# Routing work of a mixture-of-experts block at other places: ranks made at the output projection, logits and picks earlier, the late list in two pieces

## The reference

```python
sa, ca, ga, sb, cb, gb = (mod[:, 0], mod[:, 1], mod[:, 2], mod[:, 3], mod[:, 4], mod[:, 5])
ga = (2 * (ga >= 0) - 1) * jnp.maximum(jnp.abs(ga), 0.25)
gb = (2 * (gb >= 0) - 1) * jnp.maximum(jnp.abs(gb), 0.25)
h = _layernorm(x, axis=-1) * (1 + ca) + sa
x = x + ga * _L0_attn_ref(h, L0_attn_wq, L0_attn_bq, L0_attn_wk, L0_attn_bk, L0_attn_wv, L0_attn_bv, L0_attn_wo, L0_attn_bo)
h = _layernorm(x, axis=-1) * (1 + cb) + sb
x = x + gb * _L0_ffn_ref(h, L0_ffn_gate, L0_ffn_experts_w1, L0_ffn_experts_w2, L0_ffn_experts_w3)

def _L0_ffn_ref(x, gate, experts_w1, experts_w2, experts_w3):
    router_logits = jnp.einsum('bsh,he->bse', x, gate)
    routing_weights, selected = jax.lax.top_k(router_logits, TOP_K)
    routing_weights = jax.nn.softmax(routing_weights, axis=-1)
    onehot = jax.nn.one_hot(selected, E, dtype=x.dtype)
    tok_w = jnp.einsum('bsk,bske->bse', routing_weights, onehot)
    g = jnp.einsum('bsh,ehi->ebsi', x, experts_w1)
    u = jnp.einsum('bsh,ehi->ebsi', x, experts_w3)
    hid = jax.nn.silu(g) * u
    eo = jnp.einsum('ebsi,eih->ebsh', hid, experts_w2)
    return jnp.einsum('ebsh,bse->bsh', eo, tok_w)
```

## Time and profile before

| | us |
|---|---|
| median of 3 runs | 359.72 |
| lowest and highest | 357.95, 360.33 |
| profiled execution | 359.48 |
| its span, first to last instruction | 357.7 |
| mean granted clock of TensorE | 0.906 |
| TensorE, VectorE, ACT, GpSimd busy | 287.2, 217.1, 183.1, 164.9 |

### The profile page before, as it was taken

The page is one execution under the profiler, slowest core; times in us unless marked ns, Lnnn a source line. Parts: engine busy times, 40 slices in busy tenths (PEclk is TensorE's granted clock), DMA queues, the critical chain, the costliest instruction groups (busy, mean ns, idle before and its releaser), DMA issues.

```text
span 357.7 us, 7283 instructions
## 1 busy us (share of the span) xinstructions
PE 287.2 (80%) x2264; PEld 209.4 (59%) x2264; DVE 217.1 (61%) x554; ACT 183.1 (51%) x393; POOL 164.9 (46%) x262
## 2 busy tenths in 40 slices
PE   3478899999998978979785359959789999999800
PEld 2134455555554544545432149959789999999800
DVE  5668778788889796888761515882313334433227
ACT  7422476757675763656461235524526666666400
POOL 4140235455655594858649513765613333333310
PEclk9999699999999998999787659987969999999965
DMA  3932282524335342220103121543243545445355
GB/s 91 174 66 65 66 193 57 161 82 147 106 104 158 104 164 67 60 69 16 32 15 90 54 59 38 158 126 107 87 125 97 153 125 165 138 136 158 94 187 180
DMA packets 57255, 38.23 MB, mean 107 GB/s; under 512 B 5240, under 2 KB 52104, under 8 KB 57216
## 3 DMA queue, kind: packets, MB, share of 16 engines
q1 hardware_dynamic: 52880, 31.16, 32.3%
q0 software_dynamic: 2272, 4.69, 3.9%
q10 hardware_dynamic: 2064, 1.91, 2.1%
HBM read 23.58 MB, written 6.75 MB: 85 GB/s over the span
## 4 chain that ended last, share of the span: by engine, by line
PE 45%; DVE 18%; issue 12%; POOL 10%; DMA 8%; ACT 4%; ACTq 1%; SPq 1%; POOLq 0%; DVEq 0%
PE psA L1469 15%; PE psB L1479 8%; DVE negm L916 5%; PE psA L1296 4%; PE psO L1341 4%; PE psB L1321 4%; POOL xs_d L702 3%; PE psM L1276 2%; DMA y_d<-ys,qs 2%; PE psA L1299 2%; DMA xs_d<-pay,dest 2%; POOL probs L642 2%; DMA qs<-xs_d 2%; DVE xn L837 1%; PE psM L1365 1%
## 5 line engine op out<-in xcount | busy, mean ns | idle before, releaser
L480 ACT ACTIVATE probs<-psB 128x512 f32<-128x512 f32 x128 | 71.2, 594 | 35.0 <-PE psB L1321 34.7
L916 DVE TENSOR_REDUCE negm<-psA 128x4 f32<-128x1024 f32 x64 | 78.0, 1222 | 18.2 <-PE psA L1299 17.4
L1469 PE MATMUL psA<-qs,kd 128*128 128x128 f32 x624 | 81.4, 288 | 0.0
L1469 PEld LDWEIGHTS psA<-qs,kd 128*128 128x128 f32 x624 | 78.3, 204 | 0.0
L768 POOL DMA_INDIRECT y_d<-ys,qs x39 | 37.5, 962 | 77.7 <-ACT ys L552 73.2
L1169 DVE TENSOR_TENSOR qs<-psA,kd 128x512 f32<-128x512 f32 x39 | 26.9, 690 | 67.8 <-PE psA L1469 63.1
L642 POOL TENSOR_SCALAR_AFFINE_SELECT probs<-probs 128x512 f32<-128x512 f32 x64 | 39.1, 636 | 37.2 <-ACT probs L480 37.1
L1296 PE MATMUL psA<-kd,qs 96*128 96x512 bf16 x128 | 50.0, 412 | 1.7 <-DVE negm L916 1.5
L1321 PE MATMUL psB<-qs,kd 98*128 98x256 bf16 x256 | 47.3, 285 | 0.7 <-ACT probs L480 0.6
L1479 PE MATMUL psB<-kd,qs 128*128 128x128 f32 x312 | 43.7, 285 | 4.5 <-DVE qs L1169 4.0
L1479 PEld LDWEIGHTS psB<-kd,qs 128*128 128x128 f32 x312 | 40.0, 201 | 5.0 <-DVE qs L1169 5.0
(11 more groups left out here) (187 smaller groups left out, 344.8 us busy)
## 6 DMA issues: line engine op xcount, KB each, us to landing
kd<-in_L_ffn_experts_w_dram SPq DMA_DIRECT2D x39, 256.0 KB, 2.9
w_sb<-in_L_ffn_experts_w_dram SPq DMA_DIRECT2D x8, 512.0 KB, 4.5
kd<-parts SPq DMA_DIRECT2D x96, 32.0 KB
qs<-parts SPq DMA_DIRECT2D x42, 64.0 KB
mod_sb<-mod_d SPq DMA_DIRECT2D x8, 320.0 KB, 4.7
qs<-xs_d SPq DMA_DIRECT2D x39, 65.0 KB, 1.9
pay<-pay SPq DMA_DIRECT2D x8, 128.0 KB
probs<-y_d SPq DMA_DIRECT2D x3, 256.0 KB, 4.5
```

The costliest lines, as they stand in the source:

```text
L480: nc.scalar.activation(probs[:, kt, n % PRING], psB[:, kt, :].rearrange("p (h q) -> p h q", h=H2), ACT.Exp).then_inc(s["exped"], 1)
L916: nc.vector.tensor_reduce(negm[:, b % 2, :, :, j], psA[:, n % 2].rearrange("p q (h k) -> p q h k", h=H2), AX.X, ALU.max, negate=True).then ...
L1469: last = nc.tensor.matmul(ps[:, k * P:(k + 1) * P], w[:, r, k * P:(k + 1) * P], xsT[:, r], start=True, stop=True)
```

## The change

- rank_rows of sequences 0 to 3 is called inside project_out at pair 1 of steps 5 to 8, ahead of the projection's own matmuls, with other columns of the same bank (480 on; the count 496 on). Its reader is waited for together with the projection's. VectorE runs gate_attn first, then place_rows.
- In steps 6 and 7 logits are issued at pair 3 instead of 6; VectorE copies them and makes the two maxima at pair 4 and the rest (now picks) at pair 6, instead of all at pair 7. In step 8 the logits of sequence 4, its top2 and picks come at pair 2.
- The two pick instructions become one.
- GpSimd in step 8 issues put_rows of sequence 3 at pairs 2 to 5 and two of sequence 4 at pairs 6 and 7; two are left behind the loop, where five were. Between the tiles the puts come in another order around each scatter, the last of them behind scatter(8) instead of before scatter(9).
- late_list is cut in two: late_tiles at tile 6, the rest at tile 7, instead of all at tile 5.
- fill_blanks goes from step 1 to step 6 on SP.

```diff
-            return late(b)[:, 2 * E:4 * E]
+            return late(b)[:, 480:480 + 2 * E]
...
-                if step == 1:
+                if step == 6:
                     fill_blanks()
...
-                    if step == B and j in (2, 4, 6):
-                        put_rows(3, (j - 2) // 4, j // 2 % 2 ^ 1)
+                    if step == B and 2 <= j <= 5:
+                        put_rows(3, (j - 2) // 2, j % 2)
+                    if step == B and j >= 6:
+                        put_rows(4, 0, j % 2)
...
-            put_rows(3, 1, 1)
-            put_rows(4, 0, 0)
+            put_rows(4, 1, 0)
             pad_term(B - 1)
-            put_rows(4, 0, 1)
+            put_rows(4, 1, 1)
             x1_sum(B - 2)
-            put_rows(4, 1, 0)
             ln2_rstd(B - 2)
-            put_rows(4, 1, 1)
             h2_scale(B - 2)
...
+                if n == 4:
+                    weights_pow(B - 2)
+                if n == 5:
+                    weights_pow(B - 1)
                 if n == 3:
                     put_rows(B - 3, 0, 0)
...
-                if n == 8:
-                    put_rows(B - 1, 0, 1)
-                if n == 9:
-                    put_rows(B - 1, 1, 1)
-                scatter(n)
...
                 if n == 8:
                     put_rows(B - 1, 1, 0)
+                scatter(n)
...
+                if n == 7:
+                    put_rows(B - 1, 0, 1)
+                if n == 8:
+                    put_rows(B - 1, 1, 1)
...
+
+            def picks(b):
                 tt = slice(2 * b, 2 * b + 2)
...
-                for k in range(TOPK):
-                    nc.vector.tensor_tensor(pick[:, k, tt], iota_e[:].rearrange("p (o e) -> p o e", o=1).broadcast_to([P, 2, E]),
-                                            topf[:, tt, k:k + 1].broadcast_to([P, 2, E]), ALU.is_equal).then_inc(s["picks_ready"], 1)
+                nc.vector.tensor_tensor(pick[:, :, tt], iota_e[:].rearrange("p (o q e) -> p o q e", o=1, q=1).broadcast_to([P, TOPK, 2, E]),
+                                        topf[:, tt].rearrange("p t (k o) -> p k t o", o=1).broadcast_to([P, TOPK, 2, E]),
+                                        ALU.is_equal).then_inc(s["picks_ready"], 2)
...
-                    if j == 1 and 5 <= step < B:
-                        place_rows(step - 5)
                     if j == 1 and has(step - 3):
                         gate_attn(step - 3)
+                    if j == 1 and step >= 5:
+                        place_rows(step - 5)
...
-                    if j == 7 and step < B and has(step - 4):
+                    if j == (7 if step <= 5 else 4) and step < B and has(step - 4):
                         logits_copy(step - 4)
                         top2(step - 4)
+                    if j == (7 if step <= 5 else 6) and step < B and has(step - 4):
+                        picks(step - 4)
...
-                    if j == 0 and step == B:
-                        place_rows(3)
+                    if j == 2 and step == B:
                         logits_copy(4)
-                    if j == 2 and step == B:
                         top2(4)
+                        picks(4)
...
                 if n == 5:
                     place_rows(B - 1)
+                if n == 6:
+                    late_tiles()
+                if n == 7:
                     late_list()
...
-            def project_out(b):
+            def project_out(b, ranked=None):
+
                 if b == 0:
                     pe.wait_ge(s["wo_in"], 32)
-                take_late(b, ("t1_ready", 2 * b + 2))
+                if ranked is None:
+                    take_late(b, ("t1_ready", 2 * b + 2))
+                else:
+                    take_late(b, ("t1_ready", 2 * b + 2), ("rank_read", ranked + 1))
+                    rank_rows(ranked)
...
-                    if j == 1 and 5 <= step < B:
-                        rank_alone(step - 5)
                     if j == 1 and has(step - 3):
-                        project_out(step - 3)
+                        project_out(step - 3, step - 5 if step >= 5 else None)
...
-                    if j == 6 and step < B and has(step - 4):
+                    if j == (6 if step <= 5 else 3) and step < B and has(step - 4):
                         logits(step - 4)
-                    if j == 0 and step == B:
-                        logits(4, 3)
+                    if j == 2 and step == B:
+                        logits(4)
```

More of the change, by code:

```diff
@@ L227, in rank_at @@
         def rank_at(b):
-            return late(b)[:, 2 * E:4 * E]
+            return late(b)[:, 480:480 + 2 * E]
         def count_at(b):
-            return late(b)[0:1, 4 * E:5 * E]
+            return late(b)[0:1, 496:496 + E]
         xs_in = [sem(f"xs_in{r}") for r in range(XRING)]
@@ L812, in _ @@
                     put_rows(B - 1, 1, 0)
+                scatter(n)
+                if n == 3:
+                    put_rows(B - 3, 0, 1)
+                if n == 4:
+                    put_rows(B - 3, 1, 1)
+                if n == 5:
+                    put_rows(B - 2, 0, 1)
+                if n == 6:
+                    put_rows(B - 2, 1, 1)
+                if n == 7:
+                    put_rows(B - 1, 0, 1)
+                if n == 8:
+                    put_rows(B - 1, 1, 1)
         @block.vector
@@ L1095, in early_list, with late_tiles @@
                 list_done(nc.vector.tensor_tensor(taken[:, 1, 0:E], taken[:, 0, E:], taken[:, 0, E - 1:2 * E - 1], ALU.subtract))
-            def late_list():
+            def late_tiles():
                 up_to(1, count_at(B - 1))
@@ L1103, in late_list @@
                 list_done(nc.vector.tensor_tensor(tile_jump[:], tile_base[:, 1:], tile_base[:, 0:E], ALU.subtract))
+            def late_list():
                 tile_list(NEARLY, NLATE, tile_jump[:])
@@ L1191, in _ @@
             top2(B - 3)
+            picks(B - 3)
             for n in range(NTILE):
@@ L1208, in _ @@
                     top2(B - 2)
+                    picks(B - 2)
                 if n == 4:
@@ L1211, in _ @@
                     top2(B - 1)
+                    picks(B - 1)
                     place_rows(B - 2)
@@ L1378, in rank_rows @@
                 if count:
-                    nc.tensor.matmul(late(b)[:, 4 * E:5 * E], ones_b[:], before[:, 2 * b + 2], start=True, stop=True).then_inc(s["count_ps"], 1)
+                    nc.tensor.matmul(late(b)[:, 496:496 + E], ones_b[:], before[:, 2 * b + 2], start=True, stop=True).then_inc(s["count_ps"], 1)
                 nc.tensor.matmul(rank_at(b), tri[:], used[:, 2 * b:2 * b + 2].rearrange("p t e -> p (t e)"), start=True, stop=False)
@@ L1382, in rank_rows, with logits @@
                                  start=False, stop=True).then_inc(s["rank_ps"], 1)
-            def logits(b, ranked=None):
+            def logits(b):
                 pe.wait_ge(s["h2T_ready"], b + 1)
-                if ranked is None:
-                    take_late(b, ("lg_ready", b + 1))
-                else:
-                    take_late(b, ("lg_ready", b + 1), ("rank_read", ranked + 1))
+                take_late(b, ("lg_ready", b + 1))
                 for t in range(2):
@@ L1393, in logits @@
                 last.then_inc(s["lg_ps"], 1)
-                if ranked is not None:
-                    rank_rows(ranked)
             def rank_alone(b, count=False):
```

10 lines of the change are left out of this document (removed).

## The result

| | before | after |
|---|---|---|
| median of 4 runs, us | 359.51 (357.95 to 360.33) | 343.29 (342.39 to 343.65) |
| profiled execution, us | 359.48 | 343.65 |
| its span, us | 357.7 | 341.9 |
| mean granted clock of TensorE | 0.906 | 0.925 |

The ratio is 0.955, interval 0.951 to 0.959: 16.2 us faster, where 344.3 us was forecast. The total is close. Of its three terms B was met, A fell short and C came out larger, and one step of the reasoning was wrong with a visible price.

A forecast was written before the change was run, and what follows sets the result against it. No single engine was taken as the bound (TensorE carried 45% of the span); three leaks were. A 6.5 + B 5.5 - 0.3 for a landing + C 3.5 = 15.2 us, from 359.48 to 344.3 us; range 339 to 353.

The forecast's parts named there:

- B: Step 8 on GpSimd: puts moved into the loop finish the early puts sooner; 6.0 less 0.5 charged, 5.5 us gained.
- A: Attention loop, steps 5 to 8: the projection stops waiting for VectorE; 6.5 us gained at the projection of step 8.
- C: Late expert tiles: GpSimd works from scatter(3) to the last put without waiting; near 3.5 us gained.
- the first rival: Attention steps 6 and 7: VectorE keeps their length, A falls to between 1.4 and 0, 349.4 to 350.8 us; chance 0.14.
- Part (7): Attention loop: one merged pick instruction replaces two on half the elements; 0 to 0.2 us a sequence, left in A.
- The second: Late expert tiles: the late rows come no sooner, C falls to 0, 347.8 us; chance 0.10.
- The third: Step 8: paced by TensorE and ACT, not GpSimd; B falls to 2.5 us, 347.3 us; chance 0.06.
- The fourth: Expert tiles 6 to 12 and beyond: TensorE stays at 1.2 GHz, nine such tiles give 367 us; chance 0.05.

The follow-up runs named there:

- t_back: Changed kernel with logits back at pair 6, top2 and picks at pair 7 in all steps, ranks still at the projection: 338.82 us, ratio 0.955.
- b_back: Changed kernel with GpSimd's puts of step 8 in the old order, three inside the loop and five behind it: 349.19 us, ratio 0.980.
- c_back: Changed kernel with the late list in one piece at tile 5 and the puts between the tiles in the old order: 345.50 us.
- list_back: Changed kernel with only the late list back in one piece at tile 5, the new order of puts kept: 345.87 us, ratio 0.970.
- c_back2: The same kernel as c_back, measured again in another group: 345.61 us.
- a_only: Changed kernel with step 8's puts, puts between tiles, late list and blank rows' store as before; the attention part stays: 353.96 us, ratio 0.995.
- after2: The changed kernel unaltered, measured and profiled a second time: 343.06 us, ratio 0.964.
- best1: p_after with the mask of pair 7 ahead of the second put of sequence 4 in step 8: 339.33 us, ratio 0.955.
- p_after: Changed kernel with picks at pair 6 moved behind the row maximum in steps 6 and 7: 339.57 us, ratio 0.954.
- f_back: Changed kernel with fill_blanks back at step 1: 340.91 us, ratio 0.953.
- t_only: t_back with step 8's puts, puts between tiles, late list and blank rows' store also as before the change: 349.91 us, ratio 0.982.

## Why the prediction was right in the sum and wrong in a step

**Part (1), ranks at the projection: right, and undersized.** The waits for L1038 and L994 are gone as said. With the pairs left alone (t_back) the stretch from the projection of step 5 to that of step 8 shrinks from 60.7 to 52.6 us, by 8.1, where 6.5 was the term and 7.7 its upper bound. The bound counted only the summed waits and one matmul at the wrong clock; where the rest comes from was not looked into.

**Part (2), the moved pairs: the step that failed.** It was "priced at nothing", because the block "comes back as about 0.9 us before the maximum of pair 4 and 2.2 us before normalise_attn, partly in VectorE's wait for the padding term", and justified with "without this move part 1 would find the picks late, so they go together". Both halves are wrong. In step 6 the padding term was early, so the block stood on the path: it took 3.67 us instead of 2.2, TensorE waited 2.78 us for attn_T and later ran some 3.5 us (first profile; 6.4 in the second) at 1.2 GHz. Price, t_back against the changed kernel: 3.8 us at the projection of step 8 in the first profile, 5.2 in the second, 4.2 in the medians; the bound was 3.2 (1.6 in each of two steps), and in step 7 TensorE waited only 0.18 us before attn_T. And the picks would not have been late: the prediction itself had read, under (1), that they were there when the rank matmuls ran at 132.40, without asking why a projection at the same place should find them late. So of 8.1 us that A could have brought, 4.3 were left. Counted from the start of the span it is 4.6, the projection of step 8 at 170.10 us instead of 174.73 before and 168.2 forecast, because that of step 5 also came 0.4 us sooner. This is the mechanism of the first rival, VectorE keeping the length of the steps, in one step of the two.

**Part (3):** logits(4) and its top2 at pair 2 were charged 0.5 us between the projection of step 8 and GpSimd's h2_scale(5). A's 4.6 us had become 3.9 by h2_scale(5), at 183.57 us: 0.8 lost, near the charge. place_rows(3) there has two small instructions (L1044, L1030) of 1.31 and 1.35 us, which take 0.17 and 0.16 in step 6.

**Part (4), step 8 on GpSimd: right.** 10.93 us for the forecast 10.8, and b_back loses 6.1 us in the median. TensorE's tail and the landing nearly tie, as said: the first xs_T stands right behind the tail at 200.02 us without a wait for its rows, where it had waited 8.81 us in before. It was forecast at 198; the 2 us are A's.

**Part (5), late tiles: the mechanism right, the size depends on the execution.** GpSimd took 22.03 us for the forecast 21.9, the stall before down(6) was 0.42 for 1.6, down(11) came at 246.62 us, 14.6 sooner for the forecast 15. Between the first up matmul (9.6 us sooner) and down(12) (17.2 us sooner) the first profile gained 7.5 us instead of 3.5: 0.2 ahead of scatter(3), 3.4 at GpSimd, 1.2 from the last put to xs_T (the landing took 3.17 us instead of 4.26), and 2.7 because no tile at 1.2 GHz stands behind the last late rows any more (xs_T to down(12) 5.6 us before, 3.0 after). Undone in c_back and list_back the part costs only 2.5 to 2.8 us in the medians. The two don't contradict each other if what it is worth hangs on whether the clock falls behind the waits. The undone kernels fit that: counted as in the table, the span ends at 229.2 us with the clock high behind both waits (c_back), at 232.0 with it low behind one (c_back2) and at 233.5 with it low behind both (list_back). It is argued and not shown, since the last put landed at different speeds in the three too (2.89, 3.20 and 4.18 us). The parts may not be independent either: C with the blank rows' move is worth 4.8 us without B (a_only to b_back), and C 2.5 with it (c_back to after2).

So the sum of the first profile is 3.9 (A less the charge, forecast 6.0) + 5.9 (step 8 on GpSimd, forecast 6.0) - 0.1 (last early put to first up matmul, forecast -0.3) + 7.5 (C, forecast 3.5) - 1.4 (given back behind down(12), of it some 0.9 in two new waits for late rows, forecast nothing) = 15.8 us of span, forecast 15.2. An error of 2 us down and one of 4 up nearly cancelled: the total owes something to luck. By the medians of after2's group the gain was 13.9 us, on the other side of the forecast.

**Part (6), fill_blanks:** priced 0, not refuted and not shown. **Part (7):** nothing visible.

**The rivals.** The second did not come: the landing was not longer. The third, the tail, ties with the puts as the forecast said, and best1, which let it go sooner, gained 0.4 us at the first up matmul. The fourth did not come: one tile at 1.2 GHz (and part of step 6), not six or nine. The longest wait between tiles was 2.48 us, in after2 3.44.

## What to carry to other kernels

When a consumer is moved later, first ask whether its producer was ever late; if the old trace shows it ready, leave the producer where it is. A block of small VectorE instructions costs much when it stands ahead of an instruction that TensorE waits for (3.8 to 5.2 us here), and little behind a row maximum (1.0 us at most, p_after against t_back). And a gain from removing a wait of about 3 us should be given two prices, one for each clock that may follow.

## What the runs showed of the hardware

**The same wait was followed by a low clock at once in one execution and only later in another.** In after and after2, the same kernel, TensorE waited 2.78 us before attn_T in step 6. In after the two 128-column matmuls behind it took 0.44 us, the granted clock was 1.00 from 149.1 to 150.5 us and 0.53 from 150.6 to 154.1. In after2 they took 0.69 us, and the clock was 0.50 from 146.5 to 152.9; timeline of TensorE of after2:

```profile
146.54 0.69 PE L1369 MATMUL psM<-ident,attn 128*128 128x128 f32 x2 [2.78 <-DVE attn L941]
147.02 0.63 PE L1308 MATMUL psA<-kd,qs 96*128 96x512 bf16 x1
```

The difference is 1.4 us by the projection of step 8. Between expert tiles the clock stayed up behind waits of, among others, 3.08 (c_back2), 3.10 and 3.23 (c_back), 3.11 (best1), 3.17 (f_back) and 3.44 us (after2). It was down, at once or from the next group of matmuls on, behind, among others, 2.48 (after), 3.04 (a_only), 3.11 (c_back2), 3.49 (before), 3.55 (p_after) and 4.20 (list_back). The length of the wait alone does not tell which comes. The Trainium skill, "TensorE: Matmul & The Clock Gate", section HAM oscillation — how this bites in real kernels, tells of a loop that waits some 3 to 5 us for a transfer at every tile and falls to half clock at every one; here waits of 3.0 to 3.5 us did that in some executions only.

**Small VectorE instructions take longer beside some GpSimd instructions.** 8 columns twice took 2.06 us in step 6, beside a mask and the shift, and 0.36 us in the tiles (at 221.73 us), where GpSimd was issuing a put; a copy of 4 columns took 1.31 us in step 8, beside a mask of 1.24 us that started 0.02 us later, and 0.17 in step 6. That GpSimd is the cause is read from the overlap; no run here takes it away alone. The prediction, which put such a block at 2.2 us, was short by 1.5.

**The landing of one put varies by 1.9 us.** The last late put landed after 2.58 us (t_back), 2.72 (t_only), 2.89 and 3.20 (c_back, c_back2), 3.17 (after), 3.31 (b_back), 3.87 (after2), 4.12 to 4.27 (best1, a_only, list_back, before, f_back) and 4.50 (p_after), without a pattern that goes with the edits. It stands on the path that sets the end in all of these, so this alone blurs any comparison of single profiles here.

**A large store slows a put beside it.** With the blank rows' store (520 and 455 KB) in step 6, the second put of that step landed after 7.1 to 8.3 us in the seven profiles that have its landing (after, after2, b_back, c_back2, list_back, p_after, best1). With the store in step 1 it was 2.3 to 2.8 us (before, a_only, t_only, f_back). The put itself did not change, and no instruction on the path waited for it.
